# Newton-Schulz with the square completed, and the other TensorE work moved out from between its products

## The reference

```python
X = X / (sqrt(sum(X * X)) + 1e-07)
for a, b, c in NS_COEFFS:          # five triples
    A = X @ X.T
    B = b * A + c * (A @ A)
    X = a * X + B @ X
W = renorm(W + X)
```

## Time and profile before

| | |
|---|---|
| median of 3 runs | 823.1 us (822.44 to 823.59) |
| the profiled execution | 823.67 us |
| its span, first to last instruction | 821.6 us |
| mean granted TensorE clock | 0.996 of 2.4 GHz |

### The profile page before, as it was taken

How to read it: one execution, slowest core, us unless ns; L and a number is a source line. 1 busy time by engine, 2 the same in 40 slices (tenths; PEclk the granted TensorE clock), 3 DMA queues, 4 the chain that set the end, 5 groups by cost and what they waited for, 6 DMA issues and landing times.

```text
span 821.6 us, 24761 instructions
## 1 busy us (share of the span) xinstructions
PE 773.3 (94%) x9776; PEld 668.8 (81%) x9776; DVE 658.4 (80%) x2592; ACT 429.5 (52%) x996; POOL 276.4 (34%) x407
## 2 busy tenths in 40 slices
PE   3899999999999999999999999999999999999997
PEld 1878888788887888878888788887888888788886
DVE  4778788887878879888698886978879788797865
ACT  2655455454555545555545555455555554545544
POOL 1433333334333343333433334333343323433220
PEclk9899999999999999999999999999999999999999
DMA  8100000000000000000000000000000000000000
GB/s 322 57 2 15 8 2 21 3 14 8 2 21 2 14 9 2 21 2 15 8 3 20 2 15 8 3 21 2 15 8 2 21 2 15 8 2 15 2 15 7
DMA packets 9810, 15.08 MB, mean 18 GB/s; under 512 B 1120, under 2 KB 8928, under 8 KB 9440
## 3 DMA queue, kind: packets, MB, share of 16 engines
q1 hardware_dynamic: 7904, 7.80, 3.1%
q10 hardware_dynamic: 1792, 5.70, 1.8%
HBM read 11.41 MB, written 2.10 MB: 16 GB/s over the span
## 4 chain that ended last, share of the span: by engine, by line
PE 75%; ACT 15%; DVE 5%; issue 4%; DMA 1%; SPq 0%; DVEq 0%
PE CC L615 24%; PE M L615 21%; PE HB L615 13%; PE YB L615 10%; ACT hq L408 6%; DVE acc L1314 2%; ACT L556 2%; ACT XT L408 2%; DVE Am L1117 2%; DMA rows<-in_rows 1%; PE M L773 1%; ACT prT L408 1%; ACT WT L408 1%; ACT sq L408 1%; PE CC L686 1%
## 5 line engine op out<-in xcount | busy, mean ns | idle before, releaser
L340 POOL TENSOR_TENSOR aX<-X,a_tile 128x192 f32<-128x192 f32 x150 | 95.6, 658 | 177.0 <-DVE X L1132 177.0
L615 PE MATMUL YB<-e_s,hq 128*128 128x128 f32 x1024 | 141.2, 281 | 5.9 <-DVE acc L1314 5.9
L615 PE MATMUL HB<-xlT,e_s 128*128 128x128 f32 x1024 | 142.9, 283 | 0.4 <-ACT xlT L408 0.4
L408 ACT ACTIVATE hq<-HB 128x512 f32<-128x512 f32 x128 | 76.4, 597 | 121.5 <-PE HB L615 121.5
L1314 DVE SCALAR_TENSOR_TENSOR acc<-YB,cw,acc 128x128 f32<-128x128 f32 x448 | 125.5, 342 | 15.0 <-PE YB L615 15.0
L284 POOL TENSOR_TENSOR r<-r,half 128x3 f32<-128x3 f32 (+1 forms) x78 | 77.9, 1011 | 171.9 <-DVE r L1102 71.3
L615 PEld LDWEIGHTS YB<-e_s,hq 128*128 128x128 f32 x1024 | 124.2, 191 | 11.7 <-issue 8.5
L615 PEld LDWEIGHTS HB<-xlT,e_s 128*128 128x128 f32 x1024 | 126.6, 193 | 6.9 <-ACT xlT L408 0.7
L408 ACT ACTIVATE hq<-hq 128x512 f32<-128x512 f32 x128 | 80.7, 630 | 4.0
L615 PEld LDWEIGHTS CC<-Am 64*64 64x64 f32 x1800 | 60.3, 134 | 20.6 <-DVE Am L1117 15.2
L615 PE MATMUL CC<-Am 64*64 64x64 f32 x1800 | 72.6, 222 | 1.8
(11 more groups left out here) (180 smaller groups left out, 1487.8 us busy)
## 6 DMA issues: line engine op xcount, KB each, us to landing
xa<-in_x SPq DMA_DIRECT2D x16, 128.0 KB, 2.1
e_s<-in_e1T ACTq DMA_DIRECT2D x1, 2048.0 KB, 12.8
e_s<-in_e2T ACTq DMA_DIRECT2D x1, 2048.0 KB, 19.5
xr<-in_x SPq DMA_DIRECT2D x16, 128.0 KB, 2.2
out<-ot SPq DMA_DIRECT2D x16, 128.0 KB, 1.7
wall<-in_wall SPq DMA_DIRECT2D x1, 820.0 KB, 7.0
up_s<-in_upT ACTq DMA_DIRECT2D x1, 512.0 KB, 15.5
down_s<-in_downT ACTq DMA_DIRECT2D x1, 512.0 KB, 19.5
```

Of the source, the lines that this page charges most:

```text
L340: pool.tensor_tensor(aX[g][:, :, :].rearrange("p w c -> p (w c)"), X[g][:, :, :].rearrange("p w c -> p (w c)"), a_tile[:, it, :], ALU.mult ...
L408: return nc.scalar.activation(out_, in_, func, **kw)
L615: return pe.matmul(out_, lhsT, rhs, start=start, stop=stop)
```

## The change

- The square is completed. With s = b / 2c and r = a - b² / 4c, c (A + s I)² + r I equals b A + c A² + a I, so that one product with X gives the new X. Am is now A + s I, Mp is c * product + r I, and X is the plain product. GpSimd's `ax`, a_tile and the wait for them go; the tables shifts and rests come, made once by `ns_consts`.
- All three products of an iteration write the same PSUM places (`slot`), and their order and halves come from the lists GRAM, SQUARE and APPLY. Matrix w = 2 lies in the other half of the partitions after each product, except the last application.
- The fill work of all engines stands only after steps with st % 4 of 0 or 3, that is between application and turns, or between turns and gram. `h_up(i, 4)` moves from inside the gram to behind the second turn of the first iteration.
- ScalarE's `h_relu` of unit 1 moves from ahead of `w_T` in the pass before to behind `gate_sig`.

```diff
+        PROD = [CC[g][:, 0:6 * P].rearrange("p (w c) -> p w c", w=3)[:, :, 0:HD] for g in range(G)]
+        low, high = slice(0, HD), slice(HD, P)
+        GRAM = ((0, low), (2, low), (0, high), (2, high), (1, low), (1, high))
+        SQUARE = ((0, low), (0, high), (2, high), (2, low), (1, low), (1, high))
+        APPLY = ((0, low), (0, high), (2, low), (2, high), (1, low), (1, high))
+        def slot(g, w, rows):
+            return CC[g][rows, w * 2 * P:w * 2 * P + HD]
+        def other(rows):
+            return high if rows == low else low
...
-            def ax(i, g, it):
-                pool.wait_ge(e_x[g], (NI + 1) * i + it + 1)
-                pool.tensor_tensor(aX[g][:, :, :].rearrange("p w c -> p (w c)"),
-                                   X[g][:, :, :].rearrange("p w c -> p (w c)"), a_tile[:, it, :],
-                                   ALU.mult).then_inc(e_ax[g], 1)
...
@@ scalar: body @@
                 gate_sig(i)
+                h_relu(i, 1)
                 y_first(i)
...
-                fill = {1: [lambda: h_relu(i, 4)], 2: [lambda: q_out(i), lambda: prep_xnT(m)],
-                        5: [lambda: prep_qk(m)], 6: [lambda: prep_v(m)], 7: [lambda: h_relu(i, 5), lambda: prep_small(m)],
-                        8: [lambda: prep_sq8(m)], 9: [lambda: prep_vT(m), lambda: h_relu(i, 6), to_exp],
-                        11: [lambda: lr_exp(m)], 12: [lambda: prep_qkT(m)],
-                        13: [lambda: probs(i)], 14: [lambda: h_relu(i, 7), lambda: lr_ln(m)], 15: [lambda: probs_T(i), to_sigmoid],
-                        18: [lambda: comb_T(i)], 19: [lambda: x_lat(m)]}
+                fill = {0: [lambda: h_relu(i, 4)], 3: [lambda: q_out(i), lambda: prep_xnT(m)],
+                        4: [lambda: prep_qk(m)], 7: [lambda: prep_v(m), lambda: h_relu(i, 5), lambda: prep_small(m)],
+                        8: [lambda: prep_sq8(m), lambda: prep_vT(m), lambda: h_relu(i, 6), to_exp],
+                        11: [lambda: lr_exp(m)], 12: [lambda: prep_qkT(m), lambda: probs(i)],
+                        15: [lambda: h_relu(i, 7), lambda: lr_ln(m), lambda: probs_T(i), to_sigmoid],
+                        19: [lambda: comb_T(i), lambda: x_lat(m)]}
...
                 h_relu(m, 0)
                 y_T(i)
-                h_relu(m, 1)
                 for g in range(G):
                     w_T(m, g)
@@ tensor @@
+            def ns_gram(g, it):
+                xt_in[g].wait()
+                for w, c in GRAM:
+                    rows, n = (high, 1) if w == 2 else (low, w)
+                    half = other(c) if w == 2 else c
+                    ins = mm(slot(g, w, half), XT[g][rows, n, c], XT[g][rows, n, c])
+                ins.then_inc(e_prod[g], 1)
+            def ns_square(g):
+                am_in[g].wait()
+                for w, c in SQUARE:
+                    half = other(c) if w == 2 else c
+                    ins = mm(slot(g, w, c), Am[g][half, w, :], Am[g][half, w, :])
+                ins.then_inc(e_prod[g], 1)
+            def ns_apply(g, it):
+                mp_in[g].wait()
+                for w, c in APPLY:
+                    half = other(c) if w == 2 and it < NI - 1 else c
+                    ins = mm(slot(g, w, half), Mp[g][c, w, :], X[g][c, w, :])
                 ins.then_inc(e_prod[g], 1)
...
-                fill = {2: [lambda: q_out(i), lambda: prep_turn(m)], 3: [lambda: y_down(i, 2)],
-                        4: [lambda: prep_qk(m)], 5: [lambda: prep_qk_more(m)], 6: [lambda: prep_v(m)],
-                        7: [lambda: h_up(i, 5)], 8: [lambda: y_down(i, 3), lambda: prep_mom(m)],
-                        9: [lambda: prep_turn_v(m), lambda: h_up(i, 6)], 10: [lambda: y_down(i, 4)],
-                        11: [lambda: att_scores(i, False)], 12: [lambda: prep_turn_qk(m)],
-                        13: [lambda: y_down(i, 5)], 14: [lambda: h_up(i, 7)],
-                        15: [lambda: att_turn_p(i, False), lambda: y_down(i, 6)], 16: [lambda: att_pv(i)],
-                        17: [lambda: y_down(i, 7)], 18: [lambda: turn_comb(i)],
-                        19: [lambda: fc1(m), lambda: out_down(i, 0), lambda: out_down(i, 1)]}
+                fill = {3: [lambda: q_out(i), lambda: prep_turn(m), lambda: y_down(i, 2)],
+                        4: [lambda: prep_qk(m), lambda: prep_qk_more(m)], 7: [lambda: prep_v(m), lambda: h_up(i, 5)],
+                        8: [lambda: y_down(i, 3), lambda: prep_mom(m), lambda: prep_turn_v(m), lambda: h_up(i, 6)],
+                        11: [lambda: y_down(i, 4), lambda: att_scores(i, False)],
+                        12: [lambda: prep_turn_qk(m), lambda: y_down(i, 5)],
+                        15: [lambda: h_up(i, 7), lambda: att_turn_p(i, False), lambda: y_down(i, 6)],
+                        16: [lambda: att_pv(i), lambda: y_down(i, 7)],
+                        19: [lambda: turn_comb(i), lambda: fc1(m), lambda: out_down(i, 0), lambda: out_down(i, 1)]}
...
@@ vector @@
+            def ns_consts():
+                dve.wait_ge(e_ident, 16)
+                nc.vector.tensor_tensor(eye[:, :], ident[:, 0:HD], ident[:, HD:P], ALU.add).then_inc(e_eye, 1)
+                dve.wait_ge(e_eye, 1)
+                for it, (a, b, c) in enumerate(NS):
+                    nc.vector.tensor_scalar(shifts[:, it, :], eye[:, :], b / (2 * c), None, ALU.mult)
+                    nc.vector.tensor_scalar(rests[:, it, :], eye[:, :], a - b * b / (4 * c), None, ALU.mult).then_inc(e_eye, 1)
...
             def ns_a(i, g, it):
                 dve.wait_ge(e_prod[g], 3 * NI * i + 3 * it + 1)
-                nc.vector.tensor_copy(Am[g][:, :, :], CC[g][:, 0:6 * P].rearrange("p (w c) -> p w c", w=3)[:, :, 0:HD])\
+                nc.vector.tensor_tensor(Am[g][:, :, :], PROD[g], shifts[:, it, :].unsqueeze(1).to_broadcast([P, 3, HD]), ALU.add)\
                     .then_inc(e_am[g], 1)
             def ns_m(i, g, it):
-                nc.vector.scalar_tensor_tensor(Mp[g][:, :, :].rearrange("p w c -> p (w c)"),
-                                               Am[g][:, :, :].rearrange("p w c -> p (w c)"), b / c, CA[g][:, 0:3 * HD],
-                                               ALU.mult, ALU.add).then_inc(e_mp[g], 1)
+                nc.vector.scalar_tensor_tensor(Mp[g][:, :, :], PROD[g], NS[it][2],
+                                               rests[:, it, :].unsqueeze(1).to_broadcast([P, 3, HD]), ALU.mult, ALU.add)\
+                    .then_inc(e_mp[g], 1)
             def ns_x(i, g, it):
-                dve.wait_ge(e_ax[g], NI * i + it + 1)
-                nc.vector.scalar_tensor_tensor(X[g][:, :, :].rearrange("p w c -> p (w c)"), CB[g][:, 0:3 * HD], NS[it][2],
-                                               aX[g][:, :, :].rearrange("p w c -> p (w c)"), ALU.mult, ALU.add)\
-                    .then_inc(e_x[g], 1)
+                nc.vector.tensor_copy(X[g][:, :, :], PROD[g]).then_inc(e_x[g], 1)
...
-                fill = {0: [lambda: ln_norm(m), lambda: att_scale(i)], 2: [lambda: y_acc(i, 1)],
-                        3: [lambda: q_ms(i)], 4: [lambda: y_acc(i, 2)],
-                        5: [lambda: q_norm(i)], 7: [lambda: prep_silu_qk(m), lambda: prep_z(m)],
-                        8: [lambda: prep_silu_v(m), lambda: prep_ss8(m)], 9: [lambda: y_acc(i, 3), lambda: prep_mean(m)],
-                        10: [lambda: lr_a(m), lambda: prep_qkn(m)],
-                        11: [lambda: y_acc(i, 4)], 12: [lambda: att_mask(i)], 13: [lambda: att_max(i), lambda: y_acc(i, 5)],
-                        14: [lambda: lr_b(m)], 15: [lambda: y_acc(i, 6)], 16: [lambda: lr_c(m)],
-                        17: [lambda: att_out(i)], 18: [lambda: y_acc(i, 7)]}
+                fill = {0: [lambda: ln_norm(m), lambda: att_scale(i), lambda: y_acc(i, 1)],
+                        3: [lambda: q_ms(i), lambda: y_acc(i, 2)],
+                        7: [lambda: q_norm(i), lambda: prep_silu_qk(m), lambda: prep_z(m)],
+                        8: [lambda: prep_silu_v(m), lambda: prep_ss8(m), lambda: y_acc(i, 3), lambda: prep_mean(m)],
+                        11: [lambda: lr_a(m), lambda: prep_qkn(m), lambda: y_acc(i, 4)],
+                        12: [lambda: att_mask(i), lambda: att_max(i), lambda: y_acc(i, 5)],
+                        15: [lambda: lr_b(m), lambda: y_acc(i, 6)], 16: [lambda: lr_c(m), lambda: att_out(i)],
+                        18: [lambda: y_acc(i, 7)]}
```

More of the change, by code:

```diff
@@ L103, in build @@
         neghalf = sb("neghalf", [P, 8])
-        a_tile = sb("a_tile", [P, NI, 3 * HD])
+        eye = sb("eye", [P, HD])
+        shifts = sb("shifts", [P, NI, HD])
+        rests = sb("rests", [P, NI, HD])
         bdones, mask, mask_prev = fixed[:, 0, :], fixed[:, 1:3, :], fixed[:, 3, :]
@@ L208, in build @@
         e_ident = sem("ident_in")
+        e_eye = sem("eye_ready")
         e_const, e_later, e_up_w, e_down_w, e_ttw, e_init = (sem(n) for n in (
@@ L220, in build @@
```

(41 more changed lines are left out.)

## The result

The changed kernel takes 875.7 us (median of 4 runs, 875.25 to 876.87) against 823.35 for the kernel before: 1.064 times as long, 95% interval 1.062 to 1.066. I had forecast slower, 845.0 and 828 to 862, and so missed by 31 us. The profiled execution took 875.76 with a span of 873.9.

The account below looks back on a forecast made before the run. TensorE's order, busy 94%, was taken as the bound; iterations and rest summed to 52.5 us a pass against 50.96, 1.5 more, 22 us in 15 passes, giving 845.0 us, range 828 to 862.

Parts of the forecast that it names:

- Piece 1: TensorE switches between 64-wide and 128-wide products: two of three interruptions per iteration go, 0.29 us each, saving 0.57.
- The two gains: Fewer interruptions (0.57 us) and new half-array order (0.46): 1.03 per iteration, netting 0.24 where VectorE answers at once.
- piece 3: Gram, square and application merged with VectorE's answers uncovered: 2.67 us per iteration against 2.91 for today's three blocks.
- Piece 2: Square and application lists take the gram's pattern over all four array quarters: 0.23 us less each, 0.46 per iteration.
- Rival 2: Square and application don't reach the gram's pace: 1.4 us a pass more, 866 us; chance 0.08.
- Piece 4: VectorE's fills queue ahead of the Am copies, so TensorE waits: iteration 2 takes 8.49 us, iteration 3 8.20.
- Iteration 4 and rest: Last iteration to the turn of W 11.4 us against 10.56, then to the next pass 10.4 against 11.28.
- the relu: ScalarE's relu of unit 1 behind gate_sig: TensorE's 0.90 us wait for WT per pass goes.
- Iteration 0: First iteration of a pass, y_acc(1) now ahead of the first Am copy: 7.25 us against 7.32.
- Rival 1: VectorE's fills end before the gram: 3.4 us a pass of waits go, 795 us; chance 0.14 including times up to now.

Follow-up runs that it names:

- both_lists_relu: Kernel before with new lists, completed square, no GpSimd scaling and unit 1's relu behind gate_sig, all other fills in their old places; 800.3 us, ratio 0.972.
- filler: Changed kernel plus 12 unread TensorE products per pass, four in each long wait for Am in iterations 0, 2 and 3; 855.4 us, ratio 1.039.
- sq_later: Changed kernel with GpSimd's shared_sq moved from step 0 to step 3, behind rms_pow; 853.2 us, ratio 1.035.
- merged_acc_moved: Changed kernel with VectorE's y_acc(1), y_acc(3), y_acc(5) moved away from ahead of the Am copies, and shared_sq moved to step 3; 824.1 us, ratio 1.000.

## Why the prediction was right and wrong

- **Piece 1 and 3**, what merging gives and costs. Right: iteration 1 was forecast at 6.74 and measured at 6.74, from product to product 0.91. But read against the old order with the new lists (6.52) merging costs 0.22 even there. The two gains that I netted didn't need each other, which I should have said: the exposed answers of VectorE (0.63) are more than two interruptions. I had the two interruptions at 0.57 and they gave 0.41. The 0.09 at the end of a 64-wide block, for which I had no row, isn't there; my 2.91 of piece 3 had left it out, so the forecast for iteration 1 didn't suffer.
- **Piece 2**, the lists. Right in size: 0.68 to 0.71 in place of 0.92, and iteration 1 with the old fills loses 0.46. The Trainium skill's TensorEngine Tiling (Array Packing), Restrictions and Gotchas, has the rule on PSUM banks that I weighed against the trace. The new trace doesn't agree with it: SQUARE and APPLY begin with two products that read different halves and write one bank, and their 24 records run at the gram's pace (0.68 to 0.69 in `both_lists_relu`). Rival 2 didn't come.
- **Piece 4**, VectorE late. Right for iteration 2 (8.49, measured 8.49) and iteration 3 (8.20, 8.25 without the fall). Iteration 4 and rest came to 21.96 against 21.8, nearly all of it behind the turn of W (in `filler` 11.42 and 10.55, forecast 11.4 and 10.4): the relu gave 0.73 and not 0.90.
- **Iteration 0 failed as a term**: 7.25, measured 7.65. I wrote that GpSimd's "other steps only move up" and counted it as a small help. Moved up, shared_sq met xn, which stands ahead of the first Am: 1.13 in place of 0.68. That is 0.4 a pass, 6 us. `sq_later` shows it.
- **The step that failed altogether** is one that the working doesn't have. Each duration on TensorE was taken from rows at a clock of 1.00, and the sum added waits of 1.3 to 1.4 us to them as if the work around stayed as fast. The clock fell 17 times, and that is 20 us of the 31 missed. `filler` shows it from one side and `merged_acc_moved` from the other. The waits that I had forecast for iterations 2 and 3 were there to a hundredth (Am 4.67 and 3.89 after the turn, as worked out); their consequence wasn't in the range, whose upper end of 862 would have held the 855.4 of `filler`.
- The rest of the 31: iteration 0 with 6 us, the relu's 0.17 a pass with 2 to 3, iteration 3 with 1.
- **Rival 1** needed the waits under 1.9 a pass. In the changed kernel they weren't; in `merged_acc_moved`, where they were nearly all gone, the time came out at no change and not at 795. The moved accumulations then delay y_down, by 1.3 a pass of the 1.95 between 51.05 and 49.1; the rest of this wasn't followed up.

## What to carry to other kernels

Work between dependent products is cover, not clutter: before it is taken out, compare the cost of the interruption (0.20 here) with the answer of the engine between the products (0.30 here, 0.91 less TensorE's own 0.61), and with what stands in that engine's queue. When a sum adds idle time to TensorE, price its clock too, and ask of every step that an edit sets free what it will then run beside. Here the gain lay in the lists, in the place of one relu and in two accumulations put where VectorE was idle, and the merging gave it away.

## What the runs showed of the hardware

- TensorE's granted clock went to half after waits of 1.3 to 1.4 us between small products, in a kernel whose TensorE is busy for 87% of the span. With the waits filled by products that nobody reads it stayed at full, and the kernel was 20 us faster for more work.
- Two kernels can have the same time for opposite reasons: slower products and fewer falls (877.1) against faster ones and more falls (875.7). The granted clock has to be looked at before a time is read.
- 64 by 64 products that use all four quarters of the array take 0.68 to 0.69 for 24 records, those on the diagonal quarters 0.91 to 0.92, into the same PSUM places too.
- One two-input instruction on GpSimd made a VectorE instruction on SBUF of 0.41 us last 1.13; with it moved elsewhere the VectorE instruction took 0.41 again.
